# Stage zero of a decoder megakernel: row-tiled scores and per-head exponentials with bias and sum

## The reference, cut to what matters

```python
def _feature_map(x, fm_w, fm_b):
    z = jnp.einsum('nshd,ed->nshe', x, fm_w) + fm_b
    return jnp.concatenate([jnp.exp(z), jnp.exp(-z)], axis=-1)
v, k, q = (_feature_map(x, fm_w, fm_b) for x in (v, k, q))
scores = jnp.einsum('nqhd,nkhd->nhqk', q, k) / jnp.sqrt(jnp.float32(EMBED))   # EMBED = 256
attn = jax.nn.softmax(scores, axis=-1)
out = jnp.einsum('nhql,nlhd->nqhd', attn, v)
return out.reshape(N, S, HEADS * EXP_DIM) @ fc_w.T + fc_b
```

## Time and profile before

| | |
|---|---|
| median of 3 runs | 2330.02 us (2330.02 to 2331.19) |
| the profiled execution | 2332.32 us |
| its span, first to last instruction | 2330.5 us |
| TensorE busy | 2150.9 us, 92% |
| VectorE busy | 1417.5 us, 61% |
| ScalarE busy | 990.9 us, 43% |
| mean granted TensorE clock | 0.962 |

### The profile page before, as it was taken

How to read it: one execution, slowest core, us unless ns; L and a number is a source line. 1 busy time by engine, 2 the same in 40 slices (tenths; PEclk the granted TensorE clock), 3 DMA queues, 4 the chain that set the end, 5 groups by cost and what they waited for, 6 DMA issues and landing times. The chain is left out here.

```text
span 2330.5 us, 33356 instructions
## 1 busy us (share of the span) xinstructions
PE 2150.9 (92%) x12773; PEld 1527.4 (66%) x12773; DVE 1417.5 (61%) x2999; ACT 990.9 (43%) x1832; POOL 131.6 (6%) x122
## 2 busy tenths in 40 slices
PE   6996999779999699796899999999999999999988
PEld 4884998335999588555566666666666666666643
DVE  5984111673443778687566667666666676666545
ACT  5222443441111422487444444454444544444345
POOL 1002111005122000000100000000000000000000
PEclk9996999779999999898999999999999999999999
DMA  3603897123997500200000000000000000000001
GB/s 109 179 1 132 293 327 262 39 77 122 302 323 253 174 1 1 77 1 11 1 1 1 1 1 1 1 1 1 1 1 1 1 1 1 1 1 1 1 0 36
DMA packets 109257, 159.70 MB, mean 69 GB/s; under 512 B 12556, under 2 KB 85166, under 8 KB 109102
## 3 DMA queue, kind: packets, MB, share of 16 engines
q1 hardware_dynamic: 101805, 134.80, 17.7%
q0 software_dynamic: 7296, 22.78, 3.0%
HBM read 127.64 MB, written 29.91 MB: 68 GB/s over the span
## 5 line engine op out<-in xcount | busy, mean ns | idle before, releaser
L601 PE MATMUL ps<-arena,w_odd 128*128 128x128 f32 (+4 forms) x2352 | 437.8, 439 | 3.1 <-DVE arena L2059 1.2
L601 PE MATMUL ps<-arena 128*64 128x256 f32 (+4 forms) x2832 | 408.0, 390 | 7.2 <-DVE arena L2184 3.7
L2353 DVE TENSOR_REDUCE small<-ps 128x1 f32<-128x1024 f32 x256 | 312.5, 1221 | 87.2 <-PE ps L601 87.2
L601 PEld LDWEIGHTS ps<-arena 128*64 128x64 f32 (+2 forms) x2832 | 263.1, 149 | 122.6 <-issue 18.8
L1650 ACT ACTIVATE arena<-ps 128x512 f32<-128x512 f32 x256 | 139.1, 594 | 453.0 <-PE ps L1142 453.0
L601 PEld LDWEIGHTS ps<-arena,w_odd 128*128 128x128 f32 (+3 forms) x2352 | 245.9, 187 | 106.7 <-issue 101.3
L1657 ACT ACTIVATE w_odd<-ps,small 128x1101 f32<-128x1101 f32 x256 | 302.7, 1183 | 10.0 <-DVE small L2354 8.2
L1142 PEld LDWEIGHTS ps<-ident,w_odd 128*128 128x128 f32 x2048 | 222.4, 141 | 121.0 <-issue 109.8
L1142 PE MATMUL ps<-ident,w_odd 128*128 128x128 f32 x2048 | 280.8, 277 | 9.6 <-DVE arena L2294 3.1
L2371 DVE COPY arena<-ps 128x512 f32<-128x512 f32 x256 | 164.3, 683 | 4.1 <-PE ps L1142 1.8
L601 PE MATMUL ps<-xn_feat,w_even 128*128 128x512 f32 (+1 forms) x352 | 140.1, 530 | 3.0 <-DVE xn_feat L1961 2.1
(11 more groups left out here) (366 smaller groups left out, 2869.7 us busy)
## 6 DMA issues: line engine op xcount, KB each, us to landing
w_odd<-in_s_w SPq DMA_DIRECT2D x32, 1024.0 KB, 6.9
w_odd<-in_s_wgu SPq DMA_DIRECT2D x30, 704.0 KB, 5.9
w_even<-in_s_w SPq DMA_DIRECT2D x15, 1024.0 KB, 6.9
arena<-expert_rows_in SPq DMA_DIRECT2D x62, 130.0 KB, 4.4
w_odd<-in_s_wd SPq DMA_DIRECT2D x30, 256.0 KB, 3.6
out_feat<-in_s_wgu SPq DMA_DIRECT2D x10, 704.0 KB, 5.9
expert_rows_in<-zero_row POOLq DMA_DIRECT2D x1, 5070.0 KB, 34.3
vo_rows<-w_odd SPq DMA_DIRECT2D x8, 616.0 KB
```

The source lines that it names most:

```text
L601: return pe.matmul(o, lhsT, rhs, start=start, stop=stop, **kw)
L2353: link(dve.tensor_reduce(m, s6_main[h], AX.X, ALU.max, negate=True))
```

## The change

The zeros and block-diagonal keys go. VectorE makes one scaled copy `s0_kfs` of the key features (times 1/16). The scores are 16 matmuls for a tile, each of 32 partitions x 77 columns: head j of a group goes to bank j, group g to columns 77g. The banks form two halves (banks 0, 1 and banks 2, 3). VectorE takes the negated maximum of each half (`most`), ScalarE then runs eight exponentials for each half straight from PSUM, each with the head's negated maximum as bias and with the head's sum written to `at_sum`. VectorE's subtract and sum are gone in stage 0. TensorE waits for `h0_e` (both halves of the tile before) ahead of a tile's scores. Stage 4 keeps its steps, with its own counts.

```diff
-                for j in range(4):
-                    last = dve.tensor_copy(s0_kfb[32 * j:32 * j + 32, :, :, j * C:(j + 1) * C].rearrange("p b g c -> p g b c"),
-                                           s0_kf[32 * j:32 * j + 32].rearrange("p g (b c) -> p g b c", b=B))
-                last.then_inc(op0_sb, 1)
+                dve.tensor_scalar(s0_kfs, s0_kf, 1.0 / 16.0, None, ALU.mult).then_inc(op0_sb, 1)
...
-                pool.memset(s0_kfb, 0.0).then_inc(memset_done, 1)
...
+                    if t >= 1:
+                        pe.wait_ge(h0_e, 2 * t)
                     for g in range(NG):
-                        last = mm(PS[:, g, 0:GC], s0_qf[:, g, t * P:(t + 1) * P], s0_kfb[:, t // 8, g])
-                    return last
+                        for j in range(4):
+                            last = mm(PS[:, j, g * C:(g + 1) * C], s0_qf[32 * j:32 * j + 32, g, t * P:(t + 1) * P],
+                                      s0_kfs[32 * j:32 * j + 32, g, (t // 8) * C:(t // 8 + 1) * C])
+                    last.then_inc(h0_s, 1)
...
-                        act.wait_ge(at_sub, t0 + t + 1)
-                        act.activation(pr[:, t % 3], pr[:, t % 3], ACT.Exp, scale=scale).then_inc(at_exp, 1)
+                    if t < NT and s == 0:
+                        if t >= 3:
+                            act.wait_ge(at_tr, t - 2)
+                        for n in (2 * t, 2 * t + 1):
+                            act.wait_ge(h0_m, n + 1)
+                            sc = s0_half(n)
+                            for i in range(8):
+                                j, g = divmod(i, 4)
+                                h = 4 * g + 2 * (n % 2) + j
+                                last = act.activation(pr[:, t % 3, h * C:(h + 1) * C], sc[:, j, g * C:(g + 1) * C], ACT.Exp,
+                                                      bias=s0_nm[:, t % 2, n % 2, i:i + 1], accum_out=at_sum[:, t % 2, h:h + 1])
+                            last.then_inc(h0_e, 1)
...
+            def most(n):
+
+                dve.wait_ge(h0_s, n // 2 + 1)
+                dve.tensor_reduce(s0_nm[:, n // 2 % 2, n % 2].rearrange("p (j g) -> p j g", j=2),
+                                  s0_half(n).rearrange("p j (g c) -> p j g c", g=4), AX.X, ALU.max, negate=True).then_inc(h0_m, 1)
...
+                    if s == 0 and t < NT:
+                        most(2 * t)
...
+                    if t < NT and s == 0:
+                        most(2 * t + 1)
...
+                        if s == 0:
+                            dve.wait_ge(h0_e, 2 * u + 2)
+                        else:
+                            dve.wait_ge(at_exp, u + 1)
+                            link(dve.tensor_reduce(at_sum[:, q], hc, AX.X, ALU.add))
```

More of the change, by code:

```diff
@@ L110, in build @@
         s0_qf = cut(AR, 0, NG, T)
-        s0_kfb = cut(AR, 8192, B, NG, GC)
+        s0_kfs = cut(AR, 8192, NG, B * C)
         s0_vo = cut(AR, 8192 + 2464, B, NF, D)
@@ L124, in build, with s0_half @@
         at_max, at_sum, at_rec = cut(small, 0, 2, H), cut(small, 32, 2, H), cut(small, 64, 2, H)
+        s0_nm = cut(small, 0, 2, 2, 8)
+        def s0_half(n):
+            return PS[:, 2 * (n % 2):2 * (n % 2) + 2, 0:GC]
         s1_w = [(cut(r, at, KD, HID0), cut(r, at + 2048, HID0 // P, D)) for r, at in ((WO, 0), (WO, 4096), (WE, 0))]
@@ L275, in build @@
         we_in = {(s, i): sem(f"we{s}_{i}_in") for s, i in ((3, 1),)}
+        h0_s, h0_m, h0_e = sem("h0_s"), sem("h0_m"), sem("h0_e")
         at_s, at_sub, at_exp, at_p = sem("at_s"), sem("at_sub"), sem("at_exp"), sem("at_p")
@@ L667, in attention @@
             def attention(s, score, fill=None):
-                a = at_no[s]
-                t0 = NT * a
+                t0 = NT * at_no[s]
                 SCR, region, VO = (WE, SC0, s0_vo) if s == 0 else (AR, SC4, s4_vo)
@@ L678, in attention @@
                     if t < NT:
-                        if t >= 1:
-                            pe.wait_ge(at_sub, t0 + t)
-                        score(t).then_inc(at_s, 1)
+                        score(t)
                     if fill:
@@ L697, in attention @@
                         if u == 0:
-                            pe.wait_ge(vo_in, 32 if s == 0 else 64 * (a + 1))
+                            pe.wait_ge(vo_in, 32 if s == 0 else 128)
                         else:
@@ L764, in fill @@
                         pe.wait_ge(wa_in[1], 16 * 2)
-                        pe.wait_ge(at_sub, NT)
+                        pe.wait_ge(h0_e, 2 * NT)
                         for k in range(KD):
@@ L842, in score @@
                 def score(t):
+                    if t >= 1:
+                        pe.wait_ge(at_sub, t)
                     for g in range(NG):
@@ L849, in score @@
                             last = mm(PS[:, g, 0:GC], ident[:, :], s4_caus, start=False, stop=True)
-                    return last
+                    last.then_inc(at_s, 1)
                 attention(4, score)
@@ L1364, in layer_norm, with attention @@
                     logits_copy(s, 2)
-            def attention(s, scale, ahead=None, behind=None):
-                a = at_no[s]
-                t0 = NT * a
+            def attention(s, ahead=None, behind=None):
+                t0 = NT * at_no[s]
                 SCR, region = (WE, SC0) if s == 0 else (AR, SC4)
@@ L1374, in attention @@
                         ahead(t)
-                    if t < NT:
-                        act.wait_ge(at_sub, t0 + t + 1)
-                        act.activation(pr[:, t % 3], pr[:, t % 3], ACT.Exp, scale=scale).then_inc(at_exp, 1)
+                    if t < NT and s == 0:
[10 more added lines that the diff above has]
+                            last.then_inc(h0_e, 1)
+                    elif t < NT:
+                        act.wait_ge(at_sub, t + 1)
+                        act.activation(pr[:, t % 3], pr[:, t % 3], ACT.Exp, scale=DH ** -0.5).then_inc(at_exp, 1)
                     if behind:
@@ L1433, in behind @@
                             act.activation(vo_t[:, 2 + h, i:8:4], PS[0:C, 4 + i, :].rearrange("p (a d) -> p a d", a=2), ACT.Copy).then_inc(vo_sb, 1)
-                attention(0, 1.0 / 16.0, ahead, behind)
+                attention(0, ahead, behind)
                 act.wait_ge(gv_ss, 1)
@@ L1452, in stage4 @@
                 layer_norm(4)
-                attention(4, DH ** -0.5)
+                attention(4)
             def stage1():
@@ L1745, in _ @@
         def _(pool):
-            if 0 in stages:
-                pool.memset(s0_kfb, 0.0).then_inc(memset_done, 1)
             pool.memset(zero[:, :], 0.0).then_inc(memset_done, 1)
-            pool.wait_ge(memset_done, 2 if 0 in stages else 1)
+            pool.wait_ge(memset_done, 1)
             pool.wait_ge(fcb_sb, 1)
@@ L1873, in attention @@
                             dve.bn_aggr(lnmv[:, u - 1, :], lnst[:, u - 1, :])
-                    if t < NT:
+                    if t < NT and s == 0:
+                        most(2 * t + 1)
+                        if t == 0:
+                            fill()
+                    elif t < NT:
                         q = t % 2
-                        dve.wait_ge(at_s, t0 + t + 1)
+                        dve.wait_ge(at_s, t + 1)
                         sc = PS[:, 0:4, 0:GC].rearrange("p g (h c) -> p g h c", h=4)
@@ L1883, in attention @@
                                           ALU.subtract).then_inc(at_sub, 1)
-                        if fill and t == 0:
-                            fill()
                     if 2 <= t < NT + 2:
```

6 lines of the change are left out of this document (1 added, 5 removed).

## The result

| | before | changed |
|---|---|---|
| median of 10 runs each, us | 2330.68 (2329.82 to 2336.04) | 2338.21 (2335.40 to 2341.93) |
| ratio, 95% interval | | 1.003 (1.0022 to 1.0038) |
| profiled execution: time, span, us | 2332.32, 2330.5 | 2339.54, 2337.7 |
| scores of tiles 3, 4 and 15 start, us | 57.59, 66.95, 149.32 | 68.36, 78.09, 157.04 |
| steady turn (tile 4 to 15, over 11), us | 7.49 | 7.18 |

The account below looks back on a forecast made before the run. TensorE was taken to set the pace, VectorE right behind. Steady loop +22.4, first three tiles +12.5 and clock +5 made +40 us on the median of 2330.02: 2370 us, range 2345 to 2400.

Parts of the forecast that it names:

- Exponentials and scores alternate: Stage-zero loop: one set of banks, so scores wait for the previous tile's exponentials; loop 1.87 us longer than 7.48.
- The terms of the loop: Steady stage-zero tile: exponentials 6.1, scores 1.9, way to VectorE 0.46, half maximum 0.79, hand-overs 0.1, together 9.35 us.
- A pair of ACTIVATE and accumulator read: ScalarE, each 77-column exponential in stage zero: 0.38 us, so 16 take 6.1 us a tile in place of 1.23.
- The lower bound of 0.25: ScalarE's lowest price in us for a 77-column pair: bare ACTIVATE of 0.33 with an overlap and the read free.
- The scores: TensorE, 32 records a tile: 1.9 us, bounds 0.5 and 3.5, plus 0.46 from last load to VectorE's start.
- two deep: TensorE's scores: adjacent row tiles overlap by two, not four, read from a burst of 32-row matmuls; 1.75 to 2.0 us.
- Half maximum with its hand-over: VectorE's maximum over 616 columns, 0.79 us, plus hand-overs of 0.1 us, in each turn of the stage-zero loop.
- a period near 7.4 us with TensorE full: Steady stage-zero loop: the sign that would make the prediction wrong; a period of 9.3 us was expected.
- Twelve turns: Steady stage-zero loop from tile 3 to tile 15: 12 turns, each 1.87 us longer, +22.4 us.
- The first three tiles: Start of stage zero, where features share ScalarE: longer exponentials delay the next tiles' scores, +12.5 us.
- +5 for the clock: First three tiles: TensorE's waits of 4 to 5 us halve its clock, slowing scores and features, +5 us.
- the faster case: Stage zero: exponentials at 0.25 us each with four-deep scores make turns 1.4 us shorter; 2321 us, chance 7%.

Follow-up runs that it names:

- e8_addfirst: Changed kernel with VectorE's residual add ahead of the first half maximum in each stage-zero tile; 2353.6 us, ratio 1.0033 to the kernel before.
- e1_keys: Changed kernel with block-diagonal keys and 4 score matmuls of 128 x 308 a tile again, per-head exponentials kept; 2368.25 us, ratio 1.0097 to the kernel before.
- e3_jouter: Changed kernel with the score loops exchanged, so that neighbouring matmuls share a row tile; 2386.21 us, ratio 1.0161 to the kernel before.
- e5_half: Changed kernel with banks handed over by halves: scores of row tiles 0 and 1 wait for eight exponentials only; 2353.21 us, ratio 1.0029 to the kernel before.
- e4_noacc: Changed kernel without the exponentials' accumulator output, VectorE sums the tile again; 2344.55 us, ratio 1.0000 to the kernel before.
- e10_all: Changed kernel without accumulator output, first three tiles by subtract and one exponential, residual add ahead of the half maximum; 2334.34 us, ratio 0.9955 to the kernel before.
- e2_exp: Changed kernel with VectorE's subtract and sum and one 1232-column exponential again, row-tiled scores kept; 2342.99 us, ratio 0.9987 to the kernel before.

## Why the prediction was wrong

**The mechanism held, its sizes did not.** "Exponentials and scores alternate" is what the timeline shows; e8_addfirst (a wait moved and nothing won) and e1_keys (slower scores, longer turn by as much) bear it out. TensorE waits for ScalarE ahead of the scores, as was said, though 0.5 us and not 2. The steps that failed are two terms of the loop, the price of a small exponential and the price of the scores.

**The terms of the loop were too large.** Predicted 9.35 us, measured 7.16:

- *A pair of ACTIVATE and accumulator read*: 0.38 us, measured 0.30. Sixteen make 4.80 in place of 6.1, 1.3 us a turn. What failed is the line drawn from 1101 columns down to 77 (1.23 - 1024 x 0.83): the price of a column came from instructions of other lines, and 1.23 less 0.30 over 1024 columns is 0.91 ns. The lower bound of 0.25 was nearer than the value taken.
- *The scores*: 1.9 us and 0.46 to VectorE's start, measured 1.06 and 0.14, 1.16 us a turn less. The loads were priced at 0.06 to 0.11 us each, from rows where few columns move beside them, and put on the path. Here a load and its matmul pass every 0.033 us. The burst at 13.55 us held the better price: its code goes round the four row tiles in turn (L754, L785) and takes 0.10 us a record at 256 columns. An estimate from it by columns alone, 0.103 x 77 / 256, is 0.031 us a record and 1.0 us a tile. So two deep was a fair reading of that burst, and the loads set beside it were what failed; e3_jouter and e5_half show that the price hangs on the order of the row tiles. The Trainium skill (TensorE: Matmul & The Clock Gate, Part 3: Packing small matmuls) gives a speedup of 3.07 for four row tiles. The runs show 2.4 for one row tile against four in turn (0.081 to 0.033 us), and 1.9 (2.03 to 1.06 us) for this change, whose 77-column matmuls are far from the page's 512. By the page the scores would have been 0.66 us, an estimate.
- *Half maximum with its hand-over*: 0.89, as predicted (791 ns a half on average, 0.79 predicted). The hand-over back to TensorE is 0.27 us and was left out.

1.3 + 1.16 - 0.27 makes 2.19, the whole gap between 9.35 and 7.16. The prediction also named what would make it wrong, a period near 7.4 us with TensorE full; 7.18 us with TensorE busy for 19.44 of 20 us is close to that.

**Twelve turns.** The turn got shorter, so the +22.4 us became -3.4. Also, they are 11: the kernel before takes 9.36 us from tile 3 to tile 4, not 7.49, and both kernels spend that much there.

**The first three tiles.** Predicted +12.5, and +5 for the clock; measured +10.8 by the scores of tile 3. By parts for the end of the third tile's exponentials (60.8 predicted, 58.0 measured): the three sets of exponentials are 1.3 us shorter each (-3.9), the first starts at 31.59 in place of 32.69 (-1.1), the two hand-overs to TensorE cost 0.2 us more each (+0.4), and the way from scores to exponentials, of tiles 1 and 2, is 5.29 and 6.19 us where 4.75 and 4.95 were predicted at full clock (+1.8). That last term is the clock's, at most, up to there: the 5 us were 1.8. From 58.0 us to the scores of tile 3 the changed kernel takes 1.0 us more than the kernel before (10.4 for 9.3): the delay is 9.7 us at the end of the third tile's exponentials (58.0 for 48.27) and 10.8 at these scores. The rows of the changed kernel, busy times by stretch as the earlier trace rows:

```profile
42.00:47.00 5.00, 1.04 (x3) 0.19 (x1) 0.00 (x0) 5.00 (x34) 0.00 (x0) 1.00 0.00 0
47.00:53.00 6.00, 5.99 (x37) 3.49 (x38) 1.51 (x2) 2.19 (x4) 0.00 (x0) 0.52 0.00 0
```

TensorE is idle for 4 of 5 us, and the granted clock is 0.52 in the next stretch, near the lower level (1.2 GHz), as predicted. It mattered less than forecast because the exponentials fill most of the head, and they stay 0.30 us apart at either level: the third set takes 4.8 us, from 53.2 to 58.0.

**The sign and the range.** Slower was given 0.90 and it is slower, by 0.3%. But the steady loop, called the main loss, is a gain, and only the head loses. The range began at 2345 because each case in it kept the exponentials at 0.38 us, though 0.25 stood in the text as a bound; the faster case, which took both low bounds together, gave 2321 and 7%. What was missing is the middle: exponentials of 0.30 us with scores of 1.06. By the prediction's own formula that is 4.8 + 1.06 + 0.46 + 0.89 = 7.2 us, -3 in 11 turns, and with the head as measured (+10.8) 2338. That this formula meets the measured 7.16 is in part luck: the 0.46 was 0.14, and the hand-over back of 0.27 is not in it. The range should have combined the low values of two unknown prices.

## What to carry to other kernels

Where one engine must empty the banks that another fills, and there is one set of them, write the circle as a sum of starts (from issue to the reader's start, the reader's work, the hand-over back) and compare it with each engine's own work; when the two are within a few tenths, as 7.16 and 6.96 here (the second from e4_noacc, idle gaps included), a gain in one ends at the other, and only edits on both (e10_all) get through. Move a chain of small instructions off a slow engine only where that chain isn't what everybody waits for: the small exponentials cost nothing in the steady turn (7.17 us with them and 7.17 without, in e2_exp) and some 11 us over the three tiles of the head, so the old form in the first tiles and the new one later beats either. Row tiles pay when they are issued in turn, all four, and not in groups that reuse the same rows. And before two traces are compared, set their clocks side by side where the code is the same: 1.2 to 1.9 us here came from no edit.

## What was unexpected of the hardware

- The order of row-tiled matmuls is a factor of 2.4: 0.033 us a record (128-column load, 77 moving columns, 32 rows) with four row tiles in turn, 0.049 with two, 0.081 with one.
- The accumulator read costs 0.09 us of ScalarE in the chain at 77 columns, beside 0.21 for the ACTIVATE, though its record is 0.19 to 0.29 us long.
- TensorE stands idle for 0.33 us in front of each tile's 32-row loads, with nothing to wait for in the profile (every steady turn of e10_all); in front of the 128-row loads of the kernel before it doesn't.
- In the changed kernel's head, where TensorE stands idle for 4.80 us twice, the granted clock was 0.52 from 47 to 53 us, 0.84 from 53 to 58 and 0.50 from 58 to 74; e8_addfirst, with two waits of 4.8 us as well, had 1.00 again from 70 us. With waits under 1 us in each turn it stayed at 1.00. In the same code before the first scores it was 0.50 to 0.54 in three traces and 1.00 in ten. With row tiles one at a time it fell to 0.83 in a turn in which TensorE was busy throughout; why it fell there is open.
